# Expert gathers on GpSimd paced evenly over the second attention half, with one small addition behind each gather

## The reference

```python
xn = _layernorm(x)
# attention
ctx = xn @ We.T
influence = einsum('bqe,bke->bqk', ctx, ctx)
scores = einsum('bhqd,bhkd->bhqk', Q, K) * SCALE + 0.1 * influence[:, None]
attn = softmax(scores)
a = (attn @ V) @ Wo.T
# experts: the two best of eight for each row
topk_probs, topk_idx = top_k(softmax(xn @ gate_w.T), 2)
h = gelu(einsum('bsd,fed,bske->bskf', xn, w1, oh) + b1[topk_idx])
y = einsum('bskf,def,bske->bskd', h, w2, oh) + b2[topk_idx]
out = x + a + sum(y * topk_probs, over the two choices)
```

## Time and profile before

| what | value |
|---|---|
| median of 3 timed runs | 715.39 us (712.84 to 716.93) |
| span of the profiled execution, first to last instruction | 791.5 us |
| time of the profiled execution outside its span | not recorded |
| TensorE busy | 671.2 us, 85% of the span |
| VectorE busy | 619.4 us, 78% |
| ScalarE busy | 538.9 us, 68% |
| GpSimd busy | 467.2 us, 59% |
| mean granted TensorE clock | 0.958 |

### The profile page before, as it was taken

One profiled execution on the slowest core, in us unless ns is written; L12 is line 12 of the kernel. 1 busy time (PEld: TensorE's weight loads), 2 busy tenths in 40 slices (PEclk: granted clock), 3 DMA queues, 4 the chain that ended last, 5 costly groups with the idle time before them and its releaser, 6 DMA issues.

```text
span 791.5 us, 24553 instructions
## 1 busy us (share of the span) xinstructions
PE 671.2 (85%) x7800; PEld 433.1 (55%) x7800; DVE 619.4 (78%) x1106; ACT 538.9 (68%) x1123; POOL 467.2 (59%) x542
## 2 busy tenths in 40 slices
PE   0477888989889896969999999996689989988886
PEld 0463344444444443559999999993244444444444
DVE  8989878878778785948888888885587888887871
ACT  2581566776667685858888888884466766766765
POOL 8650656666566555306555565656676676676671
PEclk9997899999999998999999999999699999999998
DMA  9779545665455653664555454443376666566632
GB/s 262 253 212 299 138 125 146 154 175 158 117 159 148 176 155 100 174 111 90 101 105 102 96 109 102 103 89 100 77 153 161 159 165 166 152 161 161 159 92 61
DMA packets 162947, 113.32 MB, mean 143 GB/s; under 512 B 72624, under 2 KB 150448, under 8 KB 162864
## 3 DMA queue, kind: packets, MB, share of 16 engines
q1 hardware_dynamic: 153632, 90.63, 46.2%
q0 software_dynamic: 8192, 16.86, 8.6%
q10 hardware_dynamic: 1040, 4.76, 1.6%
HBM read 55.42 MB, written 47.19 MB: 130 GB/s over the span
## 4 chain that ended last, share of the span: by engine, by line
PE 71%; DVE 7%; issue 7%; SPq 5%; ACT 4%; another core or an unknown queue 3%; DMA 1%; ACTq 0%; DVEq 0%
PE bank L1133 20%; PE bank L1111 13%; PE bank L1251 12%; PE mx L1240 12%; PE mx L1145 7%; ACT A L708 4%; DVE mx L956 2%; PE bank L1193 2%; PE bank L1031 2%; PE bank L1162 2%; DVE A L791 2%; PE bank L1155 1%; SPq L319 1%; SPq L318 1%
## 5 line engine op out<-in xcount | busy, mean ns | idle before, releaser
L708 ACT ACTIVATE A<-bank 128x512 f32<-128x512 f32 x502 | 279.1, 602 | 109.9 <-PE bank L1133 94.1
L956 DVE TENSOR_REDUCE mx<-mx 128x4 f16<-128x1024 f32 x256 | 303.7, 1208 | 56.3 <-PE mx L1145 26.8
L1133 PE MATMUL bank<-stack 113*128 113x256 f16 x1004 | 185.2, 283 | 51.2 <-issue 24.9
L565 POOL DMA_INDIRECT slots_x<-rows,pos x128 | 123.5, 965 | 91.3 <-PE bank L1133 68.0
L579 POOL TENSOR_SCALAR rows<-rows,slot_p 128x128 f32<-128x128 f32 x142 | 112.1, 798 | 103.4 <-DVE rows L1007 103.4
L609 POOL DMA_INDIRECT rows<-slots_y,pos x128 | 121.5, 950 | 73.4 <-PE bank L1133 54.6
L1133 PEld LDWEIGHTS bank<-stack 113*128 113x128 f16 x1004 | 66.9, 99 | 164.9 <-issue 85.7
L1111 PE MATMUL bank<-A,V 128*32 128x256 f32 x2048 | 142.2, 397 | 1.7 <-ACT A L708 1.6
L752 ACT ACTIVATE rows<-mx,b 128x256 f32<-128x256 f32 x284 | 111.8, 474 | 30.0 <-PE mx L1240 30.0
L1001 DVE TENSOR_TENSOR rows<-rows 128x512 f16<-128x512 f32 x142 | 101.2, 714 | 25.2 <-ACT rows L756 22.8
L1251 PE MATMUL bank<-w,rows 128*128 x1704 | 108.2, 220 | 4.4 <-DVE rows L1001 4.4
(11 more groups left out here) (142 smaller groups left out, 616.8 us busy)
## 6 DMA issues: line engine op xcount, KB each, us to landing
stack<-ctx_rest SPq DMA_DIRECT2D x64, 256.0 KB
stack<-qk_dram SPq DMA_DIRECT2D x128, 96.0 KB
slots_y<-rows SPq DMA_DIRECT2D x71, 128.0 KB, 2.0
qk_dram<-hi_qk SPq DMA_DIRECT2D x64, 128.0 KB
stack<-ctx_high SPq DMA_DIRECT2D x128, 64.0 KB
slots_x<-A ACTq DMA_DIRECT2D x1, 4644.0 KB, 20.2
w_stage<-in_w SPq DMA_DIRECT2D x8, 512.0 KB
qk_dram<-lo_qk SPq DMA_DIRECT2D x64, 64.0 KB
```

The source lines that it names most:

```text
L565: pool.indirect_dma_start(slots_x, bass.IndirectOffsetOnAxis(pos[j][:, t:t + 1], 0), rows[:, t, :].bitcast(F32), None).then_inc(s_scat, 16)
L708: act.activation(A[:, n % NA, :, :].rearrange("p h s -> p (h s)"), scores(k, n)[:, :], ACT.Exp, scale=SCALE).then_inc(s_xp, 1)
L956: dve.tensor_reduce(mx[:, a, 8 * qt:8 * qt + 8].rearrange("q (i e w) -> q i e w", i=2, e=2)[:, :, g % 2], MX[u % 2][:, :].rearrange("q (i ...
L1133: mm = pe.matmul(scores(k, n)[:, i * S:(i + 1) * S], stack[0:SHIFT + 1, par, h, 1, c * P:(c + 1) * P], stack[0:SHIFT + 1, par, h, 0, :], s ...
```

## The change

Three things change, all in GpSimd's part of the second half.

- The number on which gather m of step n waits. It was 16 (16 + n) + 2m - 14; it becomes 260 + the whole part of 1.9375 (8n + m). The first gather moves from 242 to 260, the last one from 496 to 506.
- The addition of the choices is cut into four, one for each tile (128x128). Tile i needs gathers i and 4 + i alone. Tiles 0 and 1 are added behind gathers 6 and 7 of the same step, tiles 2 and 3 behind gathers 0 and 1 of the next.
- The addition to `x` is cut into four as well; they stand behind gathers 2 to 5 of the next step. `s_sum` now counts tiles, so VectorE waits for four times the number.

```diff
-LEAD = 8
+GSTART = 4
...
+            def add_choices(n, i):
+
+                for m in (i, 4 + i):
                     pool.wait_ge(s_yg[n % 2][m], 16 * (n // 2) + 16)
-                pool.tensor_tensor(ye2[n % 2][:, 0:4, :], ye2[n % 2][:, 0:4, :], ye2[n % 2][:, 4:8, :], ALU.add).then_inc(s_both, 1)
-
-            def add_experts(n):
-
-                pool.wait_ge(s_both, n + 1)
-                pair = halves[:, :, 2 * n:2 * n + 2, :]
-                pool.tensor_tensor(pair, pair, ye2[n % 2][:, 0:4, :].rearrange("p (h t) d -> p h t d", h=2), ALU.add).then_inc(s_sum, 1)
+                pool.tensor_tensor(ye2[n % 2][:, i, :], ye2[n % 2][:, i, :], ye2[n % 2][:, 4 + i, :], ALU.add).then_inc(s_both, 1)
+
+            def add_experts(n, i):
+
+                pool.wait_ge(s_both, 4 * n + i + 1)
+                tile = x[:, tile_of_choice(n, i), :]
+                pool.tensor_tensor(tile, tile, ye2[n % 2][:, i, :], ALU.add).then_inc(s_sum, 1)
...
-                    pool.wait_ge(s_ex, 16 * (HALF + n) + 2 * (m - LEAD) + 2)
+                    pool.wait_ge(s_ex, 16 * HALF + GSTART + (8 * n + m) * (16 * HALF - 2 * GSTART) // (8 * HALF))
                     if n >= 2:
-                        pool.wait_ge(s_sum, n - 1)
+                        pool.wait_ge(s_sum, 4 * (n - 1))
                     pool.indirect_dma_start(ye2[n % 2][:, m, :], None, slots_y, bass.IndirectOffsetOnAxis(pos[j][:, t:t + 1], 0)).then_inc(s_yg[n % 2][m], 16)
-                    if m == 3 and n:
-                        add_choices(n - 1)
-                    if m == 5 and n:
-                        add_experts(n - 1)
-            add_choices(HALF - 1)
-            add_experts(HALF - 1)
+                    if m >= 6:
+                        add_choices(n, m - 6)
+                    if m < 2 and n:
+                        add_choices(n - 1, m + 2)
+                    if 2 <= m < 6 and n:
+                        add_experts(n - 1, m - 2)
+            for i in range(2, 4):
+                add_choices(HALF - 1, i)
+            for i in range(4):
+                add_experts(HALF - 1, i)
...
-                            dve.wait_ge(s_sum, bc - HALF + 1)
+                            dve.wait_ge(s_sum, 4 * (bc - HALF) + 4)
```

More of the change, by code:

```diff
@@ L586, in _, with tile_of_choice @@
                 pool.wait_ge(sm, 16 * ((ET - i + 3) // 4))
-            halves = x[:, :, :].rearrange("p (h t) d -> p h t d", h=2)
-            def add_choices(n):
-                for m in range(8):
+            def tile_of_choice(n, i):
+                return 2 * n + i if i < 2 else 2 * (n + HALF) + i - 2
+            def add_choices(n, i):
+                for m in (i, 4 + i):
                     pool.wait_ge(s_yg[n % 2][m], 16 * (n // 2) + 16)
-                pool.tensor_tensor(ye2[n % 2][:, 0:4, :], ye2[n % 2][:, 0:4, :], ye2[n % 2][:, 4:8, :], ALU.add).then_inc(s_both, 1)
-            def add_experts(n):
-                pool.wait_ge(s_both, n + 1)
-                pair = halves[:, :, 2 * n:2 * n + 2, :]
-                pool.tensor_tensor(pair, pair, ye2[n % 2][:, 0:4, :].rearrange("p (h t) d -> p h t d", h=2), ALU.add).then_inc(s_sum, 1)
+                pool.tensor_tensor(ye2[n % 2][:, i, :], ye2[n % 2][:, i, :], ye2[n % 2][:, 4 + i, :], ALU.add).then_inc(s_both, 1)
[3 more added lines that the diff above has]
+                pool.tensor_tensor(tile, tile, ye2[n % 2][:, i, :], ALU.add).then_inc(s_sum, 1)
             for n in range(HALF):
@@ L604, in _ @@
                     j, i = m // 4, m % 4
-                    t = 2 * n + i if i < 2 else 2 * (n + HALF) + i - 2
-                    pool.wait_ge(s_ex, 16 * (HALF + n) + 2 * (m - LEAD) + 2)
+                    t = tile_of_choice(n, i)
+                    pool.wait_ge(s_ex, 16 * HALF + GSTART + (8 * n + m) * (16 * HALF - 2 * GSTART) // (8 * HALF))
                     if n >= 2:
-                        pool.wait_ge(s_sum, n - 1)
+                        pool.wait_ge(s_sum, 4 * (n - 1))
                     pool.indirect_dma_start(ye2[n % 2][:, m, :], None, slots_y, bass.IndirectOffsetOnAxis(pos[j][:, t:t + 1], 0)).then_inc(s_yg[n % 2][m], 16)
-                    if m == 3 and n:
-                        add_choices(n - 1)
-                    if m == 5 and n:
-                        add_experts(n - 1)
-            add_choices(HALF - 1)
-            add_experts(HALF - 1)
+                    if m >= 6:
[8 more added lines that the diff above has]
+                add_experts(HALF - 1, i)
         @block.scalar
```

## The result

The changed kernel is slower: a median of 723.3 us (719.2 to 724.3, 4 runs) against 714.1 (712.8 to 716.9, 4 runs), ratio 1.0114, 95% interval 1.0086 to 1.0141. Forecast was no change, 715.4 us in a range of 708 to 721.

A forecast was written before the change was run, and what follows sets the result against it. The second half's middle was taken as bound by TensorE with its ring through ScalarE and VectorE, GpSimd following. Opening 0, middle 0 and end 0 on the 715.39 us median gave 715.4 us, range 708 to 721.

The forecast's parts named there:

- A step takes 14.68 us: Middle of the second half: eight steps between output projections take 117.44 us, so TensorE's chain sets 14.68 us a step.
- the 76 us between span and median: The profiled execution was 76 us longer than the timed median of 715.39; much of its chain's gaps was attributed to recording.
- An addition costs 0.40: GpSimd's 128x128 addition, priced from L508: 0.40 us, a pair with its gather 1.53, eight pairs 12.2 us a step.
- The middle: Middle steps of the second half: VectorE's addition to `x` keeps at least 3.6 us of slack, so cost zero.
- fits by 0.2: Addition behind gather 6 comes 4.5 us after gather 4's start, against a landing of 4.33 us, so it waits for nothing.
- GpSimd becomes the bound: Rival for the second half: dearer additions or late landings make GpSimd set the pace, 719 to 734 us; chance 0.16.
- point of decision: Addition price from which GpSimd would become the bound: 0.70 us, from a step of 14.68 us.
- the upper price of L579: Upper bound for a small addition, from the median of GpSimd's 128x128 scaling at L579: 0.797 us.
- The end: Last step: the last expert result moves from 779.4 to 786.8, still 1.5 us before VectorE's last addition; cost 0.
- The opening: Start of the second half: the first gather stays at 542.22, later ones wait for counts; no gain counted, 0 us.
- the rival built on gaps of 4 to 6 us: Rival for the opening: TensorE's gaps come from twelve gathers in a row and shrink with fewer, 704 to 712 us; chance 0.18.
- The rule on shared interfaces: Skill rule that GpSimd and VectorE contend for SBUF, so spread additions might cost more; priced only as a rival.

The follow-up runs named there:

- e0: The kernel before, unchanged, profiled a second time: one run of 718.9 us, span 717.2; 23 timed runs beside it have a median of 714.9 us.
- e3: The changed kernel with each of its eight additions working on only 32 of 128 columns: 715.4 us, ratio 1.0012.
- e8: The kernel before with its old numbers, each big addition cut into four of one tile, in a row behind gathers 3 and 5: 718.0 us, ratio 1.0044.
- e5: The changed kernel's new numbers, with the two big additions kept in steps 0 to 7 and eight small ones in steps 8 to 15: 717.2 us, ratio 1.0047.
- e6: The changed kernel's new numbers, with eight small additions in steps 0 to 7 and the two big ones in steps 8 to 15: 713.8 us, ratio 0.9994.
- e1: The changed kernel's eight small additions with the old numbers of s_ex put back: 721.9 us, ratio 1.0113.
- e4: The changed kernel with each of its eight additions four places later, behind gathers 0 to 7 of the next step: 723.5 us, ratio 1.0129.
- e7: The changed kernel's new numbers with four additions a step, of two tiles (128x256) each, behind gathers 7, 1, 3 and 5: 716.1 us, ratio 1.0024.
- e2: The kernel before with only the new numbers of s_ex, its two additions of four tiles kept: 714.9 us, ratio 1.0002.

## Why the prediction was wrong

- **"A step takes 14.68 us": the step that failed.** The first profile was stretched and the true step is 13.3 us (e0). The sum compared a pair with a pace of 1.9375 counts x 14.68 / 16 = 1.78 us. The true pace is 1.9375 x 13.3 / 16 = 1.61 us. I had the 76 us between span and median in hand and put them down to gaps outside the stretches that the sum uses. The half that no edit touches shows the stretching too: in the first profile its steps (from one of VectorE's additions to the next, the last one left out) are 14.0 to 20.2 us, in e0 13.1 to 14.1.
- **"An addition costs 0.40": mis-sized.** It measured 0.464 behind a gather. A pair is 0.956 + 0.02 + 0.464 + 0.16 = 1.60 us instead of 1.53, a step of GpSimd 12.8 us instead of 12.2. The saving that the working set against it, gaps of 0.30 turned into 0.18, is there. Neither size alone would have turned the sum: a pair of 1.53 us fits into the true pace of 1.61, and one of 1.60 into the stretched 1.78.
- **The middle: "fits by 0.2".** At the true pace gather 4 is 2 x 1.60 + 0.96 = 4.16 us old when its addition comes. The 4.33 us of a landing were one wait of the stretched profile; the addition behind the last gather could start 2.7 us after it in e0 and 2.6 after the change (714.59 to 717.19). But landings spread: eleven additions of the changed kernel began only 4.3 to 5.7 us after the gather they waited for. So additions do wait (6.7 us in 12 waits), which the working had at nothing. With 1.60 against 1.61 nothing is left to work that off, and each wait and gap stays in the lag.
- **The rival "GpSimd becomes the bound" was the right one** and had 0.16. Its point of decision, 14.68 / 8 - 1.13 = 0.70 us an addition, is 13.3 / 8 - 1.13 = 0.53 by the true step, and 1.61 - 0.956 - 0.02 - 0.16 = 0.47 if GpSimd is to keep the pace of the new numbers. The addition measured 0.464: the change stands nearly on the point itself, and the upper price of L579 was not needed. From its first gather to its last GpSimd takes 211.1 us after the change and 194.0 in e0. The additions take 17.8 us more, the short gaps between instructions 10.6 less, idle time ahead of additions, nearly all of it for landings, adds 6.4, the one gap of step 14 adds 2.6 and the gathers 0.8. That the price is a needed part is shown by e3 (same order, price 0.26: 1.0012); that it costs by itself by e8 (206.3 us, without such waits and without the gap: 1.0044); that it needs steps enough to add up by e5 and e6. How the rest of the loss divides between the waits for landings and the gap no run separates.
- **The end.** The working had the last gather at 780.1 of 788.3, 8.2 us ahead of VectorE's last addition; it started at 714.6 of 719.3, and that addition then waited for GpSimd. The working let gather 2 of the last step start as soon as its number was reached; it was 11.5 us behind it. Seven small additions behind the last gather are not the main cost: e5 has them all and loses 0.47%.
- **The opening.** TensorE has no gap of over 1.2 us there in any of the later profiles, that of the unchanged kernel (e0) among them; the rival built on gaps of 4 to 6 us has nothing to stand on.
- **The rule on shared interfaces** (Trainium skill, GPSIMD Engine Reference, section Specifications): the additions spread from 452 to 479 ns only, wherever they fall in the step, so no contention of the size of L579's spread shows in this half. It is no test of the rule: by the kernel's lines none of VectorE's instructions here has two SBUF inputs, and whether one runs in a 2-port mode no row tells. Why an addition behind a gather takes 0.464 us and those of L508 0.40 is not shown; four in a row took 0.42 each in this half (e8).

Open: what the gap of 2.6 us ahead of gather 1 of step 14 is. The score tile had been there for 11 us when that gather started, and no wait of the profile explains it. It is 1.6 to 2.4 us in e1 to e4 and e7, 0.85 in e5, 2.7 in the first profile, and not there in e0, e6 and e8. It is GpSimd's 242nd indirect transfer; ahead of the 114th, 128 earlier and a scatter of the first half, every profile has 5.2 to 5.7 us of idle time. The gap alone does not slow the kernel (e2 and e3 have it), but after the change it is up to 2.6 of the 13.4 us of lag.

## What to carry to other kernels

Before a step time of a trace is set against an engine's budget, set the span against the timed median, and a stretch that no edit touches against its like; here one stretched profile turned an engine with 0.5 us of a step to spare into one with 2.5. On GpSimd the number of instructions counts: here, cutting an addition of four tiles into four raised its price from 1.28 to 1.86 us. An engine off the critical path that needs 1.60 of the 1.61 us it has is hardly off it: here its waits added up to a lag, and the lag was paid at the end of the loop.

## What the runs showed of the hardware

GpSimd's float32 addition over 128 partitions took 0.262 us for 32 columns, 0.464 for 128, 0.734 for 256 and 1.28 for 512 behind a gather: about 0.195 us and 2.1 ns a column. Four of 128 columns in a row took 1.68, 0.42 each. A gather of 128 rows kept GpSimd 0.95 to 0.96 us in the median of every run; where an addition waited for the last one, it could start 2.6 to 2.9 us after that gather's start in nine profiles, and 4.33 in the stretched one.
